# Half of each projection weight tile loaded by ScalarE's DMA queue instead of SyncE's, in a macaron transformer layer on eight cores

## The reference

```python
x = x + 0.5 * ffn(layernorm(x))
x = x + attn(layernorm(x))
x = x + 0.5 * ffn(layernorm(x))        # the same weights as the first

def ffn(x):      # W = (wq - 128) * scale[:, None], integer weights, 5632 hidden units
    return qlinear(silu(qlinear(x, gate)) * qlinear(x, up), down)

def attn(x):     # 16 heads of 128, causal, rotary embedding
    xn = rms_norm(x)
    q, k, v = xn @ wq + bq, xn @ wk + bk, xn @ wv + bv
    q, k = rope(q), rope(k)
    out = softmax(causal(q @ k.T / sqrt(128))) @ v
    return out @ wo + bo + x
```

## Time and profile before

| what | us |
|---|---|
| runs | 7251.5 and 6971.9, median 7111.7 |
| profiled execution | 6974.3 |
| its span on the slowest core (core 7) | 6972.7 |
| spans of all cores | 6920.7 to 6972.7 |

### The profile page before, as it was taken

The page is one execution under the profiler, slowest core; times in us unless marked ns, Lnnn a source line. Parts: engine busy times, 40 slices in busy tenths (PEclk is TensorE's granted clock), DMA queues, the critical chain, the costliest instruction groups (busy, mean ns, idle before and its releaser), DMA issues.

```text
span 6972.7 us, 99292 instructions; the slowest of 8 cores (6920.7 to 6972.7 us)
## 1 busy us (share of the span) xinstructions
PE 5732.5 (82%) x28160; PEld 2745.4 (39%) x28160; DVE 1426.3 (20%) x2645; ACT 923.7 (13%) x1592; POOL 365.8 (5%) x695
## 2 busy tenths in 40 slices
PE   5888898988876677676776777677689999899999
PEld 2333333433332234334433443354434444344444
DVE  3111113000000324414433232322320000200000
ACT  0000000000000022222221332142200000000000
POOL 1111100000000200100010000000000000000000
PEclk8999998999987787688888788888889999999999
DMA  6777787555555433344434142403412244222233
GB/s 107 133 133 132 147 178 153 136 128 125 130 134 159 78 100 106 80 109 122 128 81 133 35 119 82 145 20 103 99 61 76 76 120 131 80 76 79 76 117 119
DMA packets 368750, 757.79 MB, mean 109 GB/s; under 512 B 42064, under 2 KB 111184, under 8 KB 362064
## 3 DMA queue, kind: packets, MB, share of 16 engines
q1 hardware_dynamic: 188496, 461.94, 21.8%
q0 software_dynamic: 99072, 136.36, 15.1%
q10 hardware_dynamic: 80640, 153.13, 6.1%
HBM read 734.49 MB, written 153.09 MB: 127 GB/s over the span
## 4 chain that ended last, share of the span: by engine, by line
PE 61%; DMA 24%; issue 6%; DVE 5%; ACT 3%; SPq 0%; POOL 0%; DVEq 0%; ACTq 0%; POOLq 0%
PE f_pp L537 14%; PE f_pp L482 13%; PE f_pp L491 13%; DMA a_wA<-wq_sc 3%; PE a_pA L763 3%; PE a_pB L789 3%; PE a_pPV L1050 3%; DMA a_wB<-wo_sc 3%; DMA f_cvt<-wo_t 2%; PE a_pL L1057 2%; DMA f_cvt<-wq_t 2%; DMA f_cvt<-wv_t 2%; DMA f_cvt<-wk_t 2%; PE a_pA L954 2%; PE a_pB L893 2%
## 5 line engine op out<-in xcount | busy, mean ns | idle before, releaser
L482 PE MATMUL f_pp<-f_rbf,f_wg 128*128 128x512 bf16 x5632 | 1298.1, 388 | 217.1 <-DVE f_wg L448 111.7
L537 PE MATMUL f_pp<-f_g,f_wd 128*128 128x512 bf16 x5632 | 1252.4, 386 | 139.6 <-DMA f_wd<-wd_sc 107.8
L491 PE MATMUL f_pp<-f_rbf,f_wu 128*128 128x512 bf16 x5632 | 1247.3, 380 | 0.0
L482 PEld LDWEIGHTS f_pp<-f_rbf,f_wg 128*128 128x128 bf16 x5632 | 549.8, 99 | 949.3 <-issue 328.7
L537 PEld LDWEIGHTS f_pp<-f_g,f_wd 128*128 128x128 bf16 x5632 | 557.1, 99 | 834.4 <-issue 195.0
L491 PEld LDWEIGHTS f_pp<-f_rbf,f_wu 128*128 128x128 bf16 x5632 | 551.8, 98 | 667.8 <-issue 5.6
L500 DVE SCALAR_TENSOR_TENSOR f_g<-f_pp,s_su,f_gt 128x1024 bf16<-128x1024 f32 x176 | 225.9, 1284 | 2354.9 <-PE f_pp L491 1749.3
L497 ACT ACTIVATE f_gt<-f_pp,s_sg 128x1024 f32<-128x1024 f32 x176 | 196.1, 1114 | 2402.6 <-PE f_pp L482 1165.1
L893 PE MATMUL a_pB<-a_ao,a_wB 128*128 128x256 bf16 x2048 | 281.4, 295 | 113.4 <-DMA a_wB<-wo_sc 112.5
L543 DVE SCALAR_TENSOR_TENSOR f_rc<-f_pp,s_sde,f_rc 128x1024 f32<-128x1024 f32 x64 | 82.1, 1283 | 1270.6 <-PE f_pp L537 992.3
L1064 DVE RECIPROCAL a_linv<-a_pL 1x256 f32<-1x256 f32 x128 | 223.5, 1746 | 557.8 <-PE a_pL L1057 549.3
(11 more groups left out here) (128 smaller groups left out, 2942.0 us busy)
## 6 DMA issues: line engine op xcount, KB each, us to landing
f_wg<-wg_sc SPq DMA_DIRECT2D x132, 512.0 KB, 3.3
f_wu<-wu_sc SPq DMA_DIRECT2D x132, 512.0 KB, 3.4
f_wd<-wd_sc SPq DMA_DIRECT2D x48, 1408.0 KB, 9.2
a_wA<-wq_sc SPq DMA_DIRECT2D x256, 256.0 KB, 3.6
a_wB<-wo_sc SPq DMA_DIRECT2D x256, 256.0 KB, 4.5
a_wA<-wk_sc SPq DMA_DIRECT2D x128, 256.0 KB, 2.8
a_wB<-wv_sc SPq DMA_DIRECT2D x128, 256.0 KB, 2.7
f_wg<-wg_t POOLq DMA_DIRECT2D x88, 256.0 KB, 5.9
```

What stands on the lines that cost most here:

```text
L482: e.matmul(ppg[:, o:o + w], gw[:, dc * 128:(dc + 1) * 128], F.rbf[dc][:, o:o + w], start=(dc == 0), stop=(dc == NDC - 1)),
L491: e.matmul(ppu[:, o:o + w], uw[:, dc * 128:(dc + 1) * 128], F.rbf[dc][:, o:o + w], start=(dc == 0), stop=(dc == NDC - 1)),
L537: e.matmul(ppd[:, o:o + w], dw[:, hc * 128:(hc + 1) * 128], F.g[hc][:, o:o + w], start=(hc == 0), stop=(hc == NHC - 1)),
```

## The change

In the output projection and in the query projection, the second half of each weight tile is loaded by a DMA issued on ScalarE's queue; the first half stays on SyncE's. The keys' and values' projections keep both halves on SyncE's queue. The place in the written order, the buffers, the bytes and the dependencies on data stay as they are.

```diff
@@ outproj(g), for doc in range(NDC), wb = c.a_wB[par]
             for hf in range(2):
-                P.dma("qs", lambda e, doc=doc, wb=wb, hf=hf, wcols=wcols:
+                P.dma("qs" if hf == 0 else "act",
+                      lambda e, doc=doc, wb=wb, hf=hf, wcols=wcols:
                       e.dma_start(
                     wb[:, hf * wcols // 2:(hf + 1) * wcols // 2],
                     c.wo_sc[doc * 128:(doc + 1) * 128,
@@ emit_one_group(g), for i in range(NH // 2), for AB in range(2), wb = c.a_wA[par]
                 for hf in range(2):
-                    P.dma("qs", lambda e, blk=blk, wb=wb, hf=hf: e.dma_start(
+                    P.dma("qs" if hf == 0 else "act",
+                          lambda e, blk=blk, wb=wb, hf=hf: e.dma_start(
                         wb[:, hf * NDC * 64:(hf + 1) * NDC * 64],
                         c.wq_sc[blk * 128:(blk + 1) * 128,
```

## The result

The changed kernel is slower. The ratio of its time to the time before is 1.128, 95% interval 1.124 to 1.132. Counted so, the changed kernel takes 7861 to 7878 us against 6965 to 6996 us before, about +895 us. The prediction had 7781 us. The median over all 11 executions, 8270 us, lies above its range; the median over all 10 of the kernel before is 7377 us.

The account below looks back on a forecast made before the run. The prediction took both projections as bound by the latency of loads asked for one block ahead. Late second halves at low clock add 481 us (output) and 326 us (query) to 6974.3 us: 7781 us, range 7550 to 8080 us.

Parts of the forecast that it names:

- Order on ScalarE: Both projections: second half is asked for only after the previous block's matmuls, not one block ahead; with low clock, chance 0.72.
- The path to the issue: Output projection: from the previous block's last matmul through VectorE and the write's issue to the load's issue, 1.62 us.
- Landing in the output projection: Second half's load there takes 3.3 us from issue to landing, bounds 2.4 and 4.5 us.
- Query projection: Stage goes from 335.5 to 661 us, +326 us, at 5.08 us a block with a 2.8 us landing and low clock.
- Low clock in the output projection: PE's pauses drop its clock to the low level; 8 matmuls on the second half take 1.9 us, not 1.03.
- The sum: Whole kernel: output projection +481 us and query projection +326 us, 807 us on 6974.3 us, giving 7781 us.
- Nothing elsewhere: Outside the two projections: feed-forward parts and key and value projections keep their times; SP's shorter issue list brings nothing.
- The second case: Rival for both projections: same late order but PE keeps full clock, +585 us, 7559 us; chance 0.19.
- Faster: Rival for both projections: two queues land loads sooner and 191 us of PE idle time goes, 6783 us; chance 0.03.
- no change: Rival for both projections: 8 matmuls on the first half cover the second half's lateness, 6974 us; chance 0.04.
- the argument from the period: Output projection: keeping 3.08 us a block leaves 0.3 us for a landing, and none is under 2.4 us.
- The range: Whole kernel: 7550 to 8080 us, from the full-clock case up to longer landings and the full wait for the activation.

Follow-up runs that it names:

- e4: Changed kernel with ScalarE's second-half loads written two blocks ahead in its order, before the write or activation: 1.010 of before (1.005 to 1.014).
- e5: Kernel before, all loads on SyncE, second half also waiting for the previous block's last sum or activation: 7664 us, about 1.10 of before.
- e9: Changed kernel with the second half's load issued just ahead of the previous block's write on ScalarE: output projection 6.24 to 6.43 us a block.
- e7: Changed kernel without the output projection's write, the load's wait for the sum kept: output projection 5.93 to 6.16 us a block.
- e6: Changed kernel without the residual's load for 14 of 16 output-projection blocks, wait for the sum kept: 7.18 to 7.29 us a block there.
- e10: Changed kernel plus 16 matmuls per output-projection block that read the block's weight tile, between its halves: 7680 us, about 1.10 of before.
- e8: Changed kernel without the output projection's residual load and write, wait for the sum kept: 5.75 to 5.84 us a block there.
- e12: Changed kernel plus 16 matmuls per output-projection block that read no weight tile, between its halves: 7827 to 7836 us, 1.127 of before.
- e1: The changed kernel again, nothing altered, for an undisturbed profile: output projection 8.15 us a block, query projection 4.61 us a block.

## Why the prediction was right or wrong

- **Order on ScalarE: right.** The second half is asked for behind the previous block's write or activation (timeline above); e4 and e5 show that this moment, and not the second queue, makes most of the loss: early on two queues 1.010, late on one queue +710 of the +895 us.
- **The path to the issue, 1.62 us: right.** In the rows above the eighth matmul of the burst ends at 3292.28 + 1.88 = 3294.16 and the load is issued at 3295.70, 1.54 us later.
- **Landing in the output projection, 3.3 us: the step that failed.** It is 4.7 to 4.8 us, outside even the upper bound of 4.5. The prediction set it by the load on the DMA engines, which would halve, and it did halve (share 0.78 to 0.32). But the landing hangs on what stands ahead of the load in its own queue and beside it in the same microsecond. With the write behind it in place of ahead of it the load lands 1.5 to 1.7 us sooner (e9), without the write 1.8 us (e7), without the residual 0.9 us (e6), and with the first half 1.16 us behind it 1.3 us (e10). These don't add up one by one, as e8 shows: residual and write together are worth 2.1 us. 1.4 us times 120 blocks is 168 us, and the stage took 1043 us where 876 were forecast. The term was in the text ("the write and the residual start within a microsecond of it"), and got far too small a size.
- **Query projection, +326 us: too large by 71 us.** Landing 2.8 us was right (2.8 by the median). The issue comes 0.02 to 0.08 us after the activation's start, where 0.14 us was taken, and the clock did not stay low: 0.81 in the stretch, so the matmuls ran fast in some blocks (all 16 of the burst at 3430.69 take 1.91 us, no more than 8 at the low level) and slowly in others. The prediction took one level for the whole stage, and the rows show both.
- **Low clock in the output projection: right**, 0.58, and its busy time rose from 281.4 to 450.7 us. That it is on the path was right too (e12), and by the half that e12 gave back its size fits. PE's busy time in both stages rose by 258 us, above the 150 to 200 us named as a sign.
- **The sum, 7781 us against 7861 to 7878 us: close in part by luck.** The output projection was 168 us too cheap and the query projection 71 us too dear, and these two errors have opposite signs.
- **Nothing elsewhere: right.** The sum of the two stages' growth by rows, 903 us, is the whole of the measured 895 us within the difference between cores.
- **The second case (full clock, 7559 us)** did not happen in the output projection, and half happened in the query projection. **Faster** and **no change** did not; the argument from the period (0.3 us left for a landing) holds.
- **The Trainium skill's rule** that issuing engines share the DMA engines (DMA: Bandwidth & Descriptors, "Issuing engines are not separate DMA queues") agrees with e4: 1.010, no gain from the second queue.
- **The range, 7550 to 8080 us: the second step that failed.** It was made around one execution of 6974 us. The two runs shown beforehand were 280 us apart, and the prediction put that difference at nothing with the remark that the profiled one agrees with the lower. Over all executions the kernel before went to a median of 7377 us and the changed one to 8270 us, 190 us above the upper end.

## What to carry to other kernels

Each engine that issues DMAs goes through its program in order, so a load moved to another engine's queue is asked for when that engine gets there: look at what stands just ahead of it and what that waits for, before counting on a second queue. If it must go there, write it ahead of the waiting work (1.128 became 1.010), and not just behind a write that goes out at the same moment (4.8 us of landing against 3.3). Here, with loads bound by latency, more buffers on one queue were worth more than a second queue with the same buffers (0.988 against 1.010).

## What the runs showed of the hardware that was not expected

- Two neighbouring issues on one queue, a write of 128 KB in rows of 1 KB to device memory and a load of 256 KB: with the write first the load lands in 4.8 us (share of the DMA engines 0.32), with the load first in 3.3 us. Whether the rows' width, the direction or something in the queue does it was not taken apart. It takes company: with the write first but no residual it is 3.9 us, with the write first and the other queue's load 1.16 us later 3.5 us.
- ScalarE issues a DMA that follows an activation in its order 0.02 to 0.08 us after the activation has started, and doesn't wait for the 0.48 us of it.
- A load on each of two queues within 0.3 us is not slow by itself: both land late with the write ahead of one of them (4.8 and 4.7 us, e1), and 3.26 us is enough at the same distance with the write behind (e9).
